# Delta net heads 1 and 2: head 1's scores placed ahead of head 0's first cross product, and a written-out order with other PSUM banks for step 1

## The reference: what is computed

```python
qkv = hidden @ W_qkv.T;  z = hidden @ W_z.T;  a = hidden @ W_a.T;  b = hidden @ W_b.T
mixed = silu(causal_conv4(qkv, conv_w))
q, k, v = split(mixed)              # 16 key heads, each shared by 2 value heads, width 128
q = l2norm(q) * 128 ** -0.5;  k = l2norm(k)
g = -exp(A_log) * softplus(a + dt_bias);  beta = sigmoid(b)
for t in tokens:
    state = state * exp(g[t])
    delta = (v[t] - k[t] @ state) * beta[t]
    state = state + outer(k[t], delta)
    out[t] = q[t] @ state
o = out * rsqrt(mean(out ** 2) + 1e-6) * norm_w * silu(z)
x = x + o.reshape(tokens, 4096) @ W_out.T
```

## Time and profile before

| | |
|---|---|
| median of 3 runs | 1512.07 us (1511.48 to 1514.16) |
| the profiled execution: time / span of its records | 1516.13 / 1514.3 us |
| share of the span with busy PE, DVE, ACT, POOL | 93%, 72%, 40%, 39% |
| mean granted TensorE clock | 0.969 of 2.4 GHz |
| delta net, project(1, 0) to project(2, 0), "step 0" | 513.03 to 560.12 us |
| project(2, 0) to project(3, 0), "step 1" | 560.12 to 617.98 us |
| project(3, 0) to project(4, 0), "step 2" | 617.98 to 661.93 us |
| project(15, 0) starts | 1152.02 us |

### The profile page before, as it was taken

One profiled execution on the slowest core, in us unless ns is written; L12 is line 12 of the kernel. 1 busy time (PEld: TensorE's weight loads), 2 busy tenths in 40 slices (PEclk: granted clock), 3 DMA queues, 4 the chain that ended last, 5 costly groups with the idle time before them and its releaser, 6 DMA issues. The chain is left out here.

```text
span 1514.3 us, 33541 instructions
## 1 busy us (share of the span) xinstructions
PE 1409.0 (93%) x13924; PEld 975.2 (64%) x13924; DVE 1089.5 (72%) x1726; ACT 599.0 (40%) x1014; POOL 586.9 (39%) x963
## 2 busy tenths in 40 slices
PE   6999499999998868999999999999999878999999
PEld 3444278877885445777776676777667764655556
DVE  3898576688556876999898988989899645433443
ACT  2444354355324533555445545445555411111110
POOL 1021143244214645567556657755666610000000
PEclk9999799999998988999999999999999999999999
DMA  8443200110000131221222122122112205000000
GB/s 247 155 134 91 70 1 2 29 29 2 1 1 1 32 80 36 45 59 44 55 53 51 51 45 59 44 50 60 45 45 50 45 8 223 1 1 0 14 0 14
DMA packets 125959, 74.69 MB, mean 49 GB/s; under 512 B 95536, under 2 KB 107056, under 8 KB 124016
## 3 DMA queue, kind: packets, MB, share of 16 engines
q1 hardware_dynamic: 125808, 72.55, 17.9%
HBM read 54.69 MB, written 17.83 MB: 48 GB/s over the span
## 5 line engine op out<-in xcount | busy, mean ns | idle before, releaser
L1908 DVE SCALAR_TENSOR_TENSOR W<-PS,wc,W 128x504 f32<-128x504 f32 x375 | 269.4, 731 | 36.5 <-ACT W L1599 28.8
L2253 PE MATMUL PS<-HT,wgu 128*128 128x512 f32 x320 | 143.5, 592 | 0.0
L1599 ACT ACTIVATE W<-PS,wc 128x512 f32<-128x512 f32 x125 | 86.1, 690 | 119.6 <-PE PS L1284 108.9
L2387 DVE SCALAR_TENSOR_TENSOR act<-th,PS 128x512 f32<-128x512 f32 x48 | 33.0, 687 | 129.9 <-ACT th L2313 129.9
L1307 PE MATMUL PS<-wz,HT 128*128 128x256 f32 x512 | 125.0, 392 | 1.2
L1284 PE MATMUL PS<-HT,wv 128*128 128x512 f32 x252 | 122.1, 617 | 2.3 <-DVE W L1908 2.3
L1484 PE MATMUL PS<-wo,ogT 128*128 128x256 f32 x512 | 117.0, 387 | 7.3 <-DVE dl L1988 4.9
L1284 PE MATMUL PS<-HT,wkq 128*128 128x512 f32 x248 | 118.7, 621 | 3.2 <-DVE W L1908 3.2
L1484 PEld LDWEIGHTS PS<-wo,ogT 128*128 128x128 f32 x512 | 99.1, 194 | 21.9 <-DVE dl L1988 5.1
L2313 ACT ACTIVATE th<-PS 128x512 f32<-128x512 f32 x48 | 28.7, 597 | 208.2 <-PE PS L2253 208.2
L1603 ACT ACTIVATE W<-W 128x512 f32<-128x512 f32 x125 | 78.6, 629 | 74.3 <-DVE W L1908 73.0
(11 more groups left out here) (278 smaller groups left out, 2911.8 us busy)
## 6 DMA issues: line engine op xcount, KB each, us to landing
a_rows<-AT SPq DMA_DIRECT2D x16, 512.0 KB, 2.7
wk<-in_l0x_k SPq DMA_DIRECT2D x16, 384.0 KB, 5.7
wgu<-in_moe_gu SPq DMA_DIRECT2D x5, 1024.0 KB, 15.2
queries_scratch<-tts SPq DMA_DIRECT2D x32, 128.0 KB, 2.4
wkq<-in_gdn_w SPq DMA_DIRECT2D x16, 256.0 KB, 3.3
wv<-in_gdn_w SPq DMA_DIRECT2D x16, 256.0 KB, 2.8
wz<-in_gdn_w SPq DMA_DIRECT2D x16, 256.0 KB, 2.7
wo<-in_gdn_w SPq DMA_DIRECT2D x16, 256.0 KB, 2.9
```

Of the source, the lines that this page charges most:

```text
L1599: a.activation(acc[:, flows(h, q), :], PS[:, qbank(h, q), :], ACT.Copy, scale=wc[:, h % 2, 4 * c + 3:4 * c + 4]).then_inc(s["tap"], 1)
L1908: v.scalar_tensor_tensor(a0, p0, wc[:, h % 2, 4 * c + 2 - k:4 * c + 3 - k], a0, ALU.mult, ALU.add).then_inc(s["conv"], 1)
L2253: mm = pe.matmul(PS[:, 2 * (i % 2) + w, :], pack[:, k, w, :], HT[:, k, f * N:(f + 1) * N], start=(k == 0), stop=(k == DC - 1))
```

## The change

Nothing is computed otherwise. In step 0, PE issues `project(1, 5)`, `scores_q(1)` and `scores_k(1)` ahead of `cross(0)`, and `project(1, 6)` between it and `grow(0)`. DVE brings two taps of conv(1, 5) ahead of `norms`, `update(0)` behind conv(1, 5), silu(1, 5) behind `make_A`, and `keep_M` ahead of silu(1, 6). ACT follows that order.

Step 1 gets functions of its own, `second`, on PE, ACT and DVE. The first two z projections move from the end of the step to between the projections of head 2, `turn_out(0, 0)` moves behind `cross(1)` and `turn_out(0, 1)` behind `grow(1)`; project(2, 4), (2, 5) and both scores stand ahead of `cross(1)`. The z projections use banks 5, 5, 1, 1 (before 1, 1, 1, 0), and `turn_out(0, 1)` uses banks 4 and 5 (before 2 and 3). On POOL, `clear(1)` moves from ahead of `pick(3)` to ahead of `substitute(2)`. Waits follow the new banks. Steps from 2 on keep their order.

```diff
                 return (5, 7, 5, 5)[m]
+            if j == 1:
+                return (5, 5, 1, 1)[m]
             return ZB[m] if j < LAST else (1, 0, 1, 0)[m]
+
+        def tbank(g, hv):
+            return 4 if hv == 0 or g == 0 else 2
...
                     elif h > 2:
+                        if h == 3 and q == 0:
+                            pe.wait_ge(s["conv"], 72)
                         pe.wait_ge(s["z2"], h * 4 - 4)
...
                         pe.wait_ge(s["z2"], (1, 3)[m - 2])
+                    elif j == 1 and m == 0:
+                        pe.wait_ge(s["gz"], 2)
+                    elif j == 1 and m == 2:
+                        pe.wait_ge(s["conv"], 24 + 42)
+                    elif j == 1:
+                        pe.wait_ge(s["z2"], 4 + m)
                     elif j == LAST:
...
                         pe.wait_ge(s["dg"], h * 2)
-                    if h > 1:
+                    if h == 2:
+                        pe.wait_ge(s["gz"], 2)
+                    if h > 2:
                         pe.wait_ge(s["ogs"], h * 2 - 3)
...
                 def scores_k(h):
-                    if h == 1:
-                        pe.wait_ge(s["vc"], 2)
-                    if h > 1:
+                    if h == 1 or h == 2:
+                        pe.wait_ge(s["vc"], h * 2)
+                    if h > 2:
                         pe.wait_ge(s["ogs"], h * 2 - 2)
...
                         pe.wait_ge(s["z2"], 4)
+                    if j == 1:
+                        pe.wait_ge(s["ogs"], 2)
                     if j + 1 < HK:
...
                     pe.wait_ge(s[f"og{hv}"], g + 1)
-                    if hv == 1:
+                    if g == 0 and hv == 0:
+                        pe.wait_ge(s["dg"], 5)
+                        pe.wait_ge(s["z2"], 6)
+                    elif g == 0:
+                        pe.wait_ge(s["ogs"], 1)
+                    elif hv == 1:
                         if g < LAST:
...
                             pe.wait_ge(s["xa"], g * 2 - 1)
-                    b0 = 4 if hv == 0 else 2
+                    b0 = tbank(g, hv)
                     for n in range(TILES):
...
                         mm.then_inc(s["wo"], 1)
+
+                def second():
+                    project(2, 0)
+                    project(2, 1)
+                    turn_v(1, 1)
+                    decay_sums(2)
+                    project(2, 2)
+                    project_z(1, 0)
+                    project(2, 3)
+                    project_z(1, 1)
+                    project(2, 4)
+                    project(2, 5)
+                    scores_q(2)
+                    scores_k(2)
+                    cross(1)
+                    turn_out(0, 0)
+                    grow(1)
+                    project(2, 6)
+                    turn_out(0, 1)
+                    lower_cross(1)
+                    project_z(1, 2)
+                    mix(1)
+                    project(2, 7)
+                    correct(1)
+                    project_z(1, 3)
+                    outs(1)
+                    for m in range(4):
+                        project_out(0, m)
+                    turn_v(2, 0)
...
                     project(1, 4)
-                    cross(0)
+                    project(1, 5)
                     scores_q(1)
                     scores_k(1)
+                    cross(0)
+                    project(1, 6)
                     grow(0)
-                    project(1, 5)
                     lower_cross(0)
                     mix(0)
-                    project(1, 6)
                     correct(0)
...
                 first()
-                for j in range(1, LAST):
+                second()
+                for j in range(2, LAST):
                     step(j)
...
                         a.wait_ge(s["wo"], g * 2)
-                    a.activation(ogT[:, hv, :], wide(4 if hv == 0 else 2), ACT.Copy).then_inc(s["ogs"], 1)
+                    a.activation(ogT[:, hv, :], wide(tbank(g, hv)), ACT.Copy).then_inc(s["ogs"], 1)
+
+                def second():
+                    tap(2, 0)
+                    tap(2, 1)
+                    keep_v(1, 1)
+                    tanh(2, 0)
+                    tanh(2, 1)
+                    decays(2)
+                    tap(2, 2)
+                    tanh_z(1, 0)
+                    tap(2, 3)
+                    tanh(2, 2)
+                    tanh_z(1, 1)
+                    tanh(2, 3)
+                    tap(2, 4)
+                    tap(2, 5)
+                    tanh(2, 4)
+                    keep_X(1)
+                    keep_out(0, 0)
+                    tanh(2, 5)
+                    tap(2, 6)
+                    scale_wo(0)
+                    keep_out(0, 1)
+                    keep_lower(1)
+                    tanh(2, 6)
+                    tanh_z(1, 2)
+                    keep_Z(1)
+                    tap(2, 7)
+                    tanh_z(1, 3)
+                    tanh(2, 7)
+                    square_o(1, 1)
+                    square_o(1, 0)
+                    swap_scale(2)
+                    keep_v(2, 0)
...
                     tanh(1, 3)
+                    tap(1, 5)
+                    tanh(1, 4)
                     keep_X(0)
-                    tanh(1, 4)
-                    tap(1, 5)
+                    tap(1, 6)
                     tanh(1, 5)
...
                     keep_Z(0)
-                    tap(1, 6)
                     tanh(1, 6)
...
                 first()
-                for j in range(1, LAST):
+                second()
+                for j in range(2, LAST):
                     step(j)
...
                         factors(j + 1)
-                    if 0 < j and j + 1 < HK:
+                    if 1 < j and j + 1 < HK:
                         clear(j)
...
                         masked(j + 1)
+                        if j == 1:
+                            clear(1)
                         substitute(j + 1)
...
                     v.scalar_tensor_tensor(ms[:, :, :], ms[:, :, :], 1.0 / (4 * DK * DK), over(eq[:, j % 2, :], 2), ALU.mult, ALU.add).then_inc(s["ms"], 1)
+
+                def second():
+                    conv(2, 0)
+                    conv(2, 1)
+                    silu(2, 0)
+                    silu(2, 1)
+                    silu_z(1, 0)
+                    conv(2, 2)
+                    conv(2, 3)
+                    silu_z(1, 1)
+                    silu(2, 2)
+                    silu(2, 3)
+                    conv(2, 4)
+                    norm_q(2)
+                    conv_tap(2, 5, 0)
+                    conv_tap(2, 5, 1)
+                    silu(2, 4)
+                    norms(2)
+                    conv_tap(2, 5, 2)
+                    update(1)
+                    make_A(2, 0)
+                    make_A(2, 1)
+                    conv(2, 6)
+                    silu(2, 5)
+                    silu_z(1, 2)
+                    for hv in range(2):
+                        keep_M(1, hv)
+                    conv(2, 7)
+                    silu_z(1, 3)
+                    make_P(2, 0)
+                    make_P(2, 1)
+                    silu(2, 6)
+                    sum_o(1, 1)
+                    gate(1, 1)
+                    sum_o(1, 0)
+                    gate(1, 0)
+                    residual(0, 0)
+                    residual(0, 1)
+                    silu(2, 7)
+                    level(1)
...
                     norm_q(1)
+                    conv_tap(1, 5, 0)
+                    conv_tap(1, 5, 1)
                     norms(1)
+                    silu(1, 4)
+                    conv_tap(1, 5, 2)
                     update(0)
-                    silu(1, 4)
-                    conv(1, 5)
-                    silu(1, 5)
                     make_A(1, 0)
                     make_A(1, 1)
+                    silu(1, 5)
                     conv(1, 6)
+                    for hv in range(2):
+                        keep_M(0, hv)
                     silu(1, 6)
...
                     make_P(1, 1)
-                    for hv in range(2):
-                        keep_M(0, hv)
                     conv(1, 7)
...
                 first()
-                for j in range(1, LAST):
+                second()
+                for j in range(2, LAST):
                     step(j)
```

## The result

The changed kernel takes 1499.03 us, the median of 4 runs (1495.64 to 1503.68), and the kernel before 1511.78 (4 runs, 1510.41 to 1514.16): 12.75 us less, ratio 0.9916 with a 95% interval of 0.9893 to 0.9938. The forecast was 14.0 less: 1498.1, in a range from 1495.0 to 1504.5.

A forecast was written before the change was run, and what follows sets the result against it. PE bounds the kernel from step 2 on; some 14 us of step 1 are waiting or half clock. Project(3, 0) comes 14.5 earlier, less 0.5 for hand-overs: 1512.07 - 14.0 = 1498.1 us, range 1495 to 1504.5.

The forecast's parts named there:

- two ends of one chain: Steps 0 and 1: PE's 5.89 us gap is passed on, making DVE late with head 1 and POOL late for step 1.
- the 0.5 taken off for hand-overs: Sum of both steps: 14.5 us less 0.5 for hand-overs between engines that had been set to zero, giving 14.0.
- Conv(1, 7) at 550.95, project(2, 0) at 553.3, 6.8 earlier: End of step 0: conv(1, 7) follows its tap's wait for sk, and project(2, 0) waits for exactly that conv.
- A issued at 543.9, landed near 548.6, substitution from 553 to 556: Head 1's A queues behind the 1024 KB load and wkq; its blocks are read by 552.9, then POOL's substitution lasts 12.5.
- The 0.5 of slack: Step 1: least slack, at grow(1), between PE's arrival at 579.6 and TT's landing at 579.1.
- Tanh, silu, decays, tap, tanh_z and silu_z 3.5: Step 1, DVE's chain after its first two convs: these operations take 3.5 us, to 567.6.
- rival 1: Remaining PE gaps each start the next stretch at 1.2 GHz, at three places, together about 5 us: 1503.2; chance 0.18.
- The rest of DVE's chain, 28.1 to make_P's end at 595.7: Step 1 from silu_z(1, 0)'s end at 567.6: convs, norms, make_A, keep_M and make_P, after which PE resumes with project_out(0).
- rival 4: Steps 2 to 14 lock in with another phase of POOL's and DVE's work: slower, 1520 at 2.2 us each; chance 0.06.
- Rivals 2 and 3: Only step 0's saving arrives, 6.8 saved, 1505.3, chance 0.08; or nothing moves since POOL's chain holds step 2, 1512, chance 0.03.
- DVE is the chain of step 1: Step 1 from conv(2, 0) at 559.7: DVE's operations summed set the time, to make_P's end at 595.7.
- the likeliest case: PE's clock behind the gaps that stay: no fall to 1.2 GHz on the chain, so no cost.

The follow-up runs named there:

- e1: Kernel before with only step 0 reordered on PE, ACT and DVE, step 1 in its old order; ratio to before 0.9939.
- e2: Kernel before with only step 1's new order, banks, waits and moved clear(1), step 0 in its old order; ratio to before 0.9953.
- e3: Changed kernel with the 1024 KB load wg issued one step later in SP's queue; ratio to before 0.9923.
- e9: Changed kernel with wg one step later and, on ACT in step 0, tap(1, 7) and tanh(1, 7) ahead of swap_scale(1); ratio to before 0.9949.
- e11: Changed kernel run a third time, no edit, beside the version with all edits; ratio to before 0.9918.
- e4: Changed kernel with project(2, 1) issued twice, the second pass writing the same values; ratio to before 0.9929.
- e6: Changed kernel with DVE's conv(2, 2) ahead of silu_z(1, 0) and ACT's tap(2, 2) ahead of decays(2); ratio to before 0.9922.
- e0: Changed kernel run again with no edit; median 1499.75 us, ratio to before 0.9921.
- e7: Changed kernel with DVE's make_P(2) ahead of keep_M(1) in step 1; ratio to before 0.9930.
- e10: Changed kernel with wg later, tap(1, 7) ahead of swap_scale(1), conv(2, 2) first, tap(2, 2) ahead of decays(2), and make_P(2) early; ratio to before 0.9934.

## Why the prediction was right, and its misses

The forecast, its sign and its mechanism held. Of its two ends of one chain, e1 shows what the first is worth for the second: step 0 repaired takes 1.7 off the 6.33 us of waiting for `dl`, and the rest went by the new order of step 1 (e2). The size was 1.4 too large in the two steps (14.5 for the sum against 13.07). Two terms missed by 0.9 and 1.1; the 0.5 taken off for hand-overs, for which no row gave a price, hid a part of that, and that the median came within 0.9 of 1498.1 is in this part luck. Here are its own steps, on the clock of the kernel before (project(1, 4) starts 2.83 later in the changed profile, so 2.83 is taken off):

- *Project(1, 5) at 530.6, scores at 533.3, norms' end 539.9.* Measured 530.7, 533.3, 539.9.
- *`make_A(1)` done by 543.9, the tap's wait for sk until 549.8.* 543.5 and 549.8. *`grow` at 540.3 to 540.6:* 539.4.
- *Conv(1, 7) at 550.95, project(2, 0) at 553.3, 6.8 earlier.* 551.8 and 554.2, 5.9 earlier. **This term failed by 0.9**, at the sentence that `keep_M` and `make_P` fit into the pause ahead of conv(1, 7). They didn't: `lower_cross(0)` waited 2.58 for T's last four transfers, the slowest of which took 3.6 to land, and ran with `mix` at 1.2 GHz; `keep_M` waited 1.76. I had followed wg's collision only behind it in the queue (wkq, A), not ahead of it, where the profile before shows none (2.0). In e3 1.01 is left of the 2.58, and e9 shows that sk was right behind. The wait for T is not the whole of the miss: in e11 it was 2.18 with the clock up, DVE waited 1.51 for the tap and that for sk, and project(2, 0) still came at 554.0 on this clock; in e3 at 553.9. There sk was ready at 550.3 to 550.4, 0.5 later than the term has it. The gap of some 2 left ahead of project(2, 0) was 1.96 in e3 and e11, and 0.66 in the first profile, where PE itself was late.
- *A issued at 543.9, landed near 548.6, substitution from 553 to 556.* Issued at 543.5; the blocks' reads start 3.9 behind it instead of 2.6, at 547.4; substitution at 553.3. (It is 15 dependent pairs of operations, 30 in all, and not 30 pairs.)
- *`turn_out(0, 0)`'s 6.33 gone, cross(1) and grow(1) not late.* So it is, in both this profile and e2. The 0.5 of slack was never used.
- *Conv(2, 0) 8.7 behind conv(1, 7).* 8.6.
- *Tanh, silu, decays, tap, tanh_z and silu_z 3.5.* From conv(2, 1)'s end at 567.7 to silu_z's at 572.3 on its own clock, 4.6. **This term was 1.1 short**: project(2, 2) and the z projection took 5.2 instead of 3.5, for the greater part at 1.2 GHz. That is rival 1 at one of its three places, at a third of the 3.2 it had put there. In e4, at full clock, the same stretch of DVE took 3.6.
- *The rest of DVE's chain, 28.1 to make_P's end at 595.7.* From 572.3 to 599.95, 27.6. *`project_out` 6.9 and `turn_v` 0.9:* 8.0. *Project(3, 0) at 603.5:* 605.1, 12.9 earlier than before.
- *Steps 2 to 14 as before:* 533.69 against 534.04; rival 4 did not happen. Rivals 2 and 3 are excluded by the 50.92.

"DVE is the chain of step 1" was too simple. It holds up to the first z projections, but e6 shows PE a fraction of a us behind it from there to `correct(1)`: taking 1 us of idle from DVE gave 0.2.

On the clock, the likeliest case was no fall on the chain, and that was wrong in two profiles of three. All three profiles of the changed kernel show a fall in step 1 or at its start, with step 1 at 50.92, 50.90 and 50.18. Beside 50.16 in e2, the same order without a fall in the step, it cost 0.8, 0.7 and nothing; rival 1 had put some 5 on it. What decides where it falls stays open. Gaps of 2.9 to 3.1 ahead of project(2, 2) were followed by 1.2 GHz in the changed kernel, e0, e7, e9 and e10, and by 2.4 GHz in before, e1, e2 and e6. The Trainium skill, "TensorE: Matmul & The Clock Gate", section "HAM oscillation", tells of a kernel in which every burst behind a DMA wait of some 3 to 5 us starts cold. The gaps here lie at the short end of that, and the traces agree in five of these nine profiles and not in four. The length of the gap alone does not order them: behind 1.44 ahead of `lower_cross(0)` the clock fell in e10, behind 2.18 it didn't in e11. Whether the moment of a gap decides is not shown, since no run here shifts a gap alone.

## What to carry to other kernels

Where engines execute in written order, look behind a stall: here two scores stood behind a wait that they did not need, and the stall came back 40 us later as 1.7 us of another engine's lateness (e1). Sum each engine's chain to the next shared point, and name the second latest as well; a repaired wait is worth only the distance to it, which was under 1 us at two places here (e3, e6). When single runs spread more than the edit is worth, compare the starts of the same instruction in two profiles, ahead of and behind the edit, and then once more far behind it: e10's 0.6 to 1.7 was gone there.

## What the runs showed of the hardware

- The same code can leave PE at 1.2 GHz for a short or a long stretch. With waits of 2.4 to 2.9 ahead of `lower_cross(0)`, the low clock ended with `mix` in the changed kernel (project(1, 7) 1.98) and with project(1, 7) in e6 and e4 (3.64 and 3.66), and step 0 took 41.0 or 43.7 and 43.8.
- Four transfers issued directly ahead of a 1024 KB load in one queue can land late, though they were issued first: the slowest took 3.2 to 3.8 in seven of the eight profiles with the new order of step 0 and the load behind them, 2.0 to 2.5 in the three with the load moved away, and 2.0 in the two with the load and the old order.
- With no edit ahead of it, project(1, 0) started anywhere from 508.71 to 518.65 in 13 profiles; most of the spread between runs is made before the edited steps. In the three profiles of the changed kernel the spans differ by 7.3 (1498.0 to 1505.3), and the spans from project(1, 0) on by 1.6 (985.8 to 987.4).
